# A vision tower with two experts per token: where the experts' rows are put in token order

## The reference, cut to what matters

```
x = _ln(mv + x, ln2_g, ln2_b)
logits = x @ gate_w + gate_b
topv, topi = jax.lax.top_k(logits, 2)
probs = jax.nn.softmax(topv, axis=-1)
w = jnp.sum(jax.nn.one_hot(topi, 8) * probs[..., None], axis=-2)
h = jax.nn.gelu(jnp.einsum('bsd,edf->ebsf', x, e_w1) + e_b1)
ye = jnp.einsum('ebsf,efd->ebsd', h, e_w2) + e_b2
moe = jnp.einsum('ebsd,bse->bsd', ye, w)
x = _ln(moe + x, ln3_g, ln3_b)
```

## Time and profile before

| | us |
|---|---|
| median of the runs (3329.47 to 3344.37) | 3334.4 |
| the profiled execution | 3318.28 |
| its span, first to last instruction | 3316.4 |
| TensorE busy (matmul) | 2775.0 |
| TensorE weight loads | 2181.5 |
| DVE busy | 1901.2 |
| ScalarE busy | 1843.2 |
| POOL busy | 1134.6 |

### The profile page before, as it was taken

How to read it: one execution, slowest core, us unless ns; L and a number is a source line. 1 busy time by engine, 2 the same in 40 slices (tenths; PEclk the granted TensorE clock), 3 DMA queues, 4 the chain that set the end, 5 groups by cost and what they waited for, 6 DMA issues and landing times.

```text
span 3316.4 us, 69976 instructions
## 1 busy us (share of the span) xinstructions
PE 2775.0 (84%) x25687; PEld 2181.5 (66%) x25687; DVE 1901.2 (57%) x4527; ACT 1843.2 (56%) x3725; POOL 1134.6 (34%) x964
## 2 busy tenths in 40 slices
PE   6999999999999859999996677877788777877787
PEld 4766666666666549999995456655566555655565
DVE  4878878878788742222221355655565555655566
ACT  4777777777777734444443345544454444544454
POOL 1454555655555530000002533333333333333310
PEclk9999999999999979999998688887888888878888
DMA  3222222222222137777774111111111111111110
GB/s 119 88 84 72 96 83 72 101 78 75 100 76 73 42 114 228 228 230 227 230 228 140 34 40 41 29 41 44 44 40 27 43 44 43 40 28 44 44 30 26
DMA packets 139758, 287.14 MB, mean 87 GB/s; under 512 B 25440, under 2 KB 82784, under 8 KB 135392
## 3 DMA queue, kind: packets, MB, share of 16 engines
q1 hardware_dynamic: 114912, 245.68, 22.9%
q0 software_dynamic: 24576, 37.80, 4.2%
...
## 4 chain that ended last, share of the span: by engine, by line
PE 47%; issue 7%; another core or an unknown queue 4%; DVE 3%; ACT 1%; POOL 1%; DMA 0%; SPq 0%; DVEq 0%; ACTq 0%; POOLq 0%
PE psum L1174 8%; PE psum L1165 8%; PE psum L1538 7%; PE psum L1498 5%; PE psum L1555 3%; PE psum L1568 3%; PE psum L1523 2%; PE psum L1503 2%; PE psum L1580 2%; DVE qdiag L1837 1%; PE psum L1598 1%; PE psum L1156 1%; PE psum L1546 1%; DVE inv L1852 1%
## 5 line engine op out<-in xcount | busy, mean ns | idle before, releaser
L1466 POOL DMA_INDIRECT ycho<-expert_out,place x384 | 367.5, 957 | 1417.4 <-DVE place L1829 1309.7
L1208 ACT ACTIVATE hid<-psum,w_blk 128x256 f32<-128x256 f32 x608 | 269.1, 474 | 326.2 <-PE psum L1165 326.2
L1039 POOL DMA_INDIRECT expert_in<-rows,slot_i x384 | 392.3, 1022 | 133.2 <-issue 111.6
L1852 DVE RECIPROCAL inv<-psum 128x64 f32<-128x64 f32 x288 | 159.5, 554 | 464.7 <-remote 385.9
L1538 PE MATMUL psum<-keys,qdiag 64*64 64x80 f32 x4608 | 281.4, 256 | 124.1 <-issue 123.7
L1752 ACT ACTIVATE ex<-psum,smin 128x80 f32<-128x80 f32 x1152 | 282.2, 332 | 142.9 <-DVE smin L1845 135.8
L1538 PEld LDWEIGHTS psum<-keys,qdiag 64*64 64x64 f32 x4608 | 214.8, 148 | 211.1 <-issue 195.7
L502 PE MATMUL psum<-xn,w_in 128*128 128x288 f32 x1024 | 311.1, 429 | 39.6 <-DVE xn L861 10.2
L1174 PE MATMUL psum<-w_blk,hid 128*128 128x128 f32 x2432 | 296.6, 275 | 0.0
L1568 PE MATMUL psum<-ex_t,pair_ones 128*32 128x64 f32 x4608 | 137.8, 244 | 189.6 <-DVE half L1853 124.0
L1165 PE MATMUL psum<-x_t,w_blk 128*128 128x256 f32 x1216 | 289.5, 381 | 2.4 <-DMA w_blk<-w_exp_in 2.4
...
## 6 DMA issues: line engine op xcount, KB each, us to landing
w_blk<-w_exp_in SPq DMA_DIRECT2D x152, 578.0 KB, 3.8
...
rows_in<-expert_in SPq DMA_DIRECT2D x152, 128.0 KB, 2.3
expert_out<-rows_out SPq DMA_DIRECT2D x152, 128.0 KB, 3.0
...
```

Of the source, the lines that this page charges most:

```text
L1039: pool.indirect_dma_start(out=expert_in[:, :], out_offset=bass.IndirectOffsetOnAxis(ap=slot_i[z.s][:, n:n + 1], axis=0), in_=rows[z.s][:, ...
L1208: nc.scalar.activation(hid[b.s][:, c, :], HB[b.s][c % HK], ACT.Gelu_apprx_tanh, bias=w_blk[b.q][:, FF + FC * D + c:FF + FC * D + c + 1]).t ...
L1466: pool.indirect_dma_start(out=ycho[x.s][:, k, :], out_offset=None, in_=expert_out[:, :], in_offset=bass.IndirectOffsetOnAxis(ap=place[x.s] ...
L1852: v.reciprocal(inv[:], sum_bank()).then_inc(head_step, 1)
```

## The change

1. A row in `expert_in` grows from 128 to 132 floats: the token's number, its first expert, and its two weights stand behind the data. POOL writes the token number (a small operation ahead of each item's scatters) and also waits for the weights.
2. The ranks come from three products: DVE forms a running sum over the six groups (a scan in place of the reduction), and one product with it replaces five.
3. The table load at L688 is made once, ahead of the steps.
4. In the expert stage DVE works out for each row of a block its weight (`share`) and its place by token (`dest`: first choices, then second choices, then a dump area for unused rows), adds the bias into `sums_y` and scales into `rows_out` (two operations). POOL stores each block by two indirect DMAs of 128 rows of 512 bytes; SP no longer stores. SP's load of a block's rows also waits for `dest`.
5. In the last stage the rows lie in token order: SP loads them with two plain DMAs for each item, ahead of its other work of the step; POOL's gather and multiplication, DVE's `place`, and the `out_rows` chain are gone. POOL only adds.

The diff, cut to its core:

```diff
-        expert_in = nc.dram_tensor("expert_in", (E * REGION + BLK, D), F32, kind="Internal").ap()
-        expert_out = nc.dram_tensor("expert_out", (NB * BLK, D), F32, kind="Internal").ap()
+        expert_in = nc.dram_tensor("expert_in", (E * REGION + BLK, RW), F32, kind="Internal").ap()
+        expert_out = nc.dram_tensor("expert_out", (3 * tokens + 2 * BLK, D), F32, kind="Internal").ap()
...
             def ranks(z, bank):
 
-                pe.wait_ge(route_step, z.upto(ROUTE, 13))
+                pe.wait_ge(route_step, z.upto(ROUTE, 15))
                 if z.old(1):
                     pe.wait_ge(chosen_new, z.upto(1, 0))
                 dst = rank_bank(bank)
-                nc.tensor.matmul(dst, C("before")[0:G, :], picks[z.s][:], start=True, stop=False)
-                for g in range(NG - 1):
-                    nc.tensor.matmul(dst[:, g + 1:NG, :], C("ones")[0:G, 0:G],
-                                     picks[z.s][:, g:g + 1, :].to_broadcast([G, NG - 1 - g, E]),
-                                     start=False, stop=False)
+                nc.tensor.matmul(dst, C("before")[0:G, :], by_group(picks[z.s][:]), start=True, stop=False)
+                nc.tensor.matmul(dst, C("ones")[0:G, 0:G], by_group(upto_g[z.s][:]), start=False, stop=False)
                 nc.tensor.matmul(dst, C("ones")[0:G, 0:G], chosen[:].unsqueeze(1).to_broadcast([G, NG, E]),
                                  start=False, stop=True).then_inc(rank_done, 1)
...
         def a_scalar(act):
             a_prep_scalar(act)
             act.wait_ge(consts_ready, 4)
+            act.preload_act_table_set("gelu_apprx_tanh_and_others")
...
             def step(x, y, z, w):
 
 
-                act.preload_act_table_set("gelu_apprx_tanh_and_others")
...
         def route_pairs(v, z):
             s = z.s
             route_after(v, z, 12)
-            v.tensor_tensor(picks[s][:], pick1[s][:], pick2[s][:], ALU.add).then_inc(route_step, 1)
+            v.tensor_tensor(by_group(picks[s][:]), pick1[s][:], pick2[s][:], ALU.add).then_inc(route_step, 1)
             v.tensor_tensor(wexp[s][:], top2[s][:], top1[s][:], ALU.subtract).then_inc(route_step, 1)
             route_after(v, z, 13)
-            v.tensor_reduce(newly[s][:], picks[s][:].rearrange("p g e -> p e g"), AX_X, ALU.add
-                            ).then_inc(route_step, 1)
+            v.tensor_tensor_scan(upto_g[s][:], within[:], picks[s][:], 0.0, ALU.mult, ALU.add).then_inc(route_step, 1)
...
                 if z:
+                    if z.old(2):
+                        pool.wait_ge(scattered[z.s], 16 * 2 * NG * z.n)
+                    pool.tensor_scalar(rows[z.s][:, :, TOKEN], C("token")[0:G, :], float((2 * z.n + z.s) * T), None,
+                                       ALU.add).then_inc(token_ready, 1)
+                    hold(pool, token_ready, z.upto(1, 1))
                     hold(pool, rows_ready, z.upto(2, 2))
                     hold(pool, slots_ready, z.upto(1, 1))
+                    hold(pool, route_step, z.upto(ROUTE, ROUTE))
                     for choice in range(2):
...
-            def store(b):
-                hold(sp, rows_out_ready[b.s], b.k + 1)
-                sp.dma_start(expert_out[bass.DynSlice(b.n * BLK, BLK), :].rearrange("(p c) d -> p (c d)", c=CB),
-                             rows_out[b.s][:].rearrange("p c d -> p (c d)")).then_inc(block_stored[b.s], 16)
-
             for q in range(BR):
                 load(Block(0, q))
             with sp.Fori(1, GROUPS) as i:
                 for q in range(BR):
-                    store(Block(i - 1, q))
                     load(Block(i, q))
-            for q in range(BR):
-                store(Block(GROUPS - 1, q))
-            for s in range(2):
-                sp.wait_ge(block_stored[s], 16 * (NB // 2))
+
+        def b_pool(pool):
+            def store(b):
+                hold(pool, dest_ready[b.s], b.k + 1)
+                hold(pool, rows_out_ready[b.s], b.k + 1)
+                for c in range(CB):
+                    pool.indirect_dma_start(
+                        out=expert_out[:, :], out_offset=bass.IndirectOffsetOnAxis(ap=dest[b.s][:, c:c + 1], axis=0),
+                        in_=rows_out[b.s][:, c, :], in_offset=None).then_inc(block_stored[b.s], 16)
+
+            with pool.Fori(0, GROUPS) as i:
+                for q in range(BR):
+                    store(Block(i, q))
 
...
             def turn_in(b):
                 pe.wait_ge(r_landed[b.q], 16 * b.i + 16)
                 if not b.first():
-                    pe.wait_ge(rows_out_ready[b.s], b.k)
+                    pe.wait_ge(sums_ready[b.s], b.k)
                 for c in range(CB):
-                    last = nc.tensor.transpose(TB[b.s][:, c * 128:(c + 1) * 128], rows_in[b.q][:, c, :], C("ident"))
+                    last = nc.tensor.transpose(TB[b.s][:, c * 128:(c + 1) * 128], rows_in[b.q][:, c, 0:D], C("ident"))
                 last.then_inc(in_turned[b.s], 1)
...
+            def shares(b):
+                expert = w_blk[b.q][:, WCOLS - 1:WCOLS]
+                first_pick = rows_in[b.q][:, :, FIRST]
+                v.wait_ge(r_landed[b.q], 16 * b.i + 16)
+                v.wait_ge(w_landed[b.q], 16 * b.i + 16)
+                v.tensor_scalar(second[b.s][:], first_pick, expert, float(tokens), ALU.not_equal, ALU.mult
+                                ).then_inc(share_step[b.s], 1)
+                v.scalar_tensor_tensor(out=share0[b.s][:], in0=first_pick, scalar=expert, in1=rows_in[b.q][:, :, W0],
+                                       op0=ALU.is_equal, op1=ALU.mult).then_inc(share_step[b.s], 1)
+                v.scalar_tensor_tensor(out=share1[b.s][:], in0=first_pick, scalar=expert, in1=rows_in[b.q][:, :, W1],
+                                       op0=ALU.not_equal, op1=ALU.mult).then_inc(share_step[b.s], 1)
+                if b.s:
+                    v.tensor_scalar(unused[:], first_pick, 0.0, float(BLK), ALU.is_equal, ALU.mult).then_inc(unused_step, 1)
+                    v.wait_ge(unused_step, 2 * b.k + 1)
+                    v.wait_ge(share_step[b.s], 4 * b.k + 1)
+                    v.tensor_tensor(second[b.s][:], second[b.s][:], unused[:], ALU.add).then_inc(unused_step, 1)
+                    v.wait_ge(unused_step, 2 * b.k + 2)
+                if not b.first():
+                    v.wait_ge(block_stored[b.s], 16 * CB * b.k)
+                v.wait_ge(share_step[b.s], 4 * b.k + 3)
+                v.tensor_tensor(share[b.s][:], share0[b.s][:], share1[b.s][:], ALU.add).then_inc(share_step[b.s], 1)
+                v.tensor_tensor(dest[b.s][:], rows_in[b.q][:, :, TOKEN], second[b.s][:], ALU.add
+                                ).then_inc(dest_ready[b.s], 1)
+
             def block(b, final=False):
                 if not final:
                     take_in(following(b))
+                shares(b)
                 v.wait_ge(y_done[b.s], b.k + 1)
-                if not b.first():
-                    v.wait_ge(block_stored[b.s], 16 * b.k)
-                v.tensor_tensor(rows_out[b.s][:], YB[b.s].rearrange("p (c d) -> p c d", c=CB),
-                                w_blk[b.q][:, WCOLS - D:WCOLS].unsqueeze(1).to_broadcast([128, CB, D]), ALU.add
-                                ).then_inc(rows_out_ready[b.s], 1)
+                v.tensor_tensor(sums_y[b.s][:], YB[b.s].rearrange("p (c d) -> p c d", c=CB),
+                                w_blk[b.q][:, WCOLS - 1 - D:WCOLS - 1].unsqueeze(1).to_broadcast([128, CB, D]), ALU.add
+                                ).then_inc(sums_ready[b.s], 1)
+                v.wait_ge(share_step[b.s], 4 * b.k + 4)
+                v.wait_ge(sums_ready[b.s], b.k + 1)
+                for c in range(CB):
+                    last = v.tensor_scalar(rows_out[b.s][:, c, :], sums_y[b.s][:, c, :], share[b.s][:, c:c + 1], None,
...
                 still(t)
 
         def c_sync(sp):
+            for s in range(2):
+                sp.wait_ge(block_stored[s], 16 * CB * (NB // 2))
+
             def load(x):
                 if x.old(2):
                     hold(sp, h2_ready, x.upto(1, -1))
                 sp.dma_start(h1c[x.s][:], h1_dram[:, a_range(x.n, x.s)]).then_inc(h_landed[x.s], 16)
                 sp.dma_start(x2c[x.s][:], x2_dram[:, a_range(x.n, x.s)]).then_inc(h_landed[x.s], 16)
+                if x.old(2):
+                    hold(sp, ysum_step, x.upto(1, -1))
+                for choice in range(2):
+                    sp.dma_start(ycho[x.s][:, choice, :, :].rearrange("p g d -> p (g d)"),
+                                 expert_out[choice * tokens + (2 * x.n + x.s) * T:choice * tokens + (2 * x.n + x.s + 1) * T,
+                                            :].rearrange("(p g) d -> p (g d)", g=NG)).then_inc(gathered[x.s], 16)
...
@@ -1454,36 +1495,16 @@
                 sp.wait_ge(out_stored[s], 16 * ITERS)
 
         def c_pool(pool):
-            for s in range(2):
-                pool.wait_ge(block_stored[s], 16 * (NB // 2))
```

(20 more changed lines are left out.)

112 lines of the change are left out of this document (54 added, 58 removed).

## The result

| | before | after |
|---|---|---|
| median of four runs, us | 3335.1 (3329.5 to 3344.4) | 2971.6 (2967.4 to 2977.2) |
| the profiled execution, us | 3318.3 | 2971.0 |

The ratio is 0.891, 95% interval 0.888 to 0.893: 11% faster. The forecast was 3010 us, with a range from 2865 to 3170. Against the profiled execution the sum had 2997 us, and that execution took 2971.

A forecast was written before the change was run, and what follows sets the result against it. TensorE was taken as the bound, busy throughout the expert stage and held back by POOL's strings of indirect DMAs elsewhere. 3318.3 - 418 - 17 + 0 + 114 = 2997, with 16 for the median 3013, given as 3010 us; range 2865 to 3170.

The forecast's parts named there:

- Last stage, steady steps: 29 steps of the last stage lose their gathers and fall from 46.34 to 31.9 us each: -418 us.
- The mechanism: A string of POOL's indirect DMAs lets about 45 TensorE matmuls through, then holds TensorE until the string has landed.
- Into the last stage: From the last expert block to the first transposes, 12.2 us in place of 29.2: -17 us.
- First stage: 31 steps, 0.4 us saved on ranks against 0.4 us of scatter delay: 0, with cases of +10 and -12 us.
- between 0.15 us and 0.6 us, I take 0.4: First stage: delay of POOL's scatters by the small token operation and a wait, counted in full each step.
- "-0.4" for the ranks: First stage: three products in place of seven save 0.7 us, less 0.3 us for the later scan.
- the table load: First stage: the 1.28 us load has ScalarE's wait behind it while TensorE embeds the next item: 0.
- Expert stage: Two scatters per block make TensorE wait 1.5 us for every two blocks: +114 us, from 0 to 245.
- "fits": Expert stage: DVE's added 1.9 us beside its 0.85 us fits within the 3.73 us of a block.
- Rival A: Expert stage: TensorE isn't held, 0 in place of +114, whole 2899 us; chance 0.30.
- Rival C: Expert stage: TensorE stands still during each scatter, 643 us in place of 114, whole 3542 us, beyond 6.6 us per block; chance 0.07.

The follow-up runs named there:

- plain_in_before: The kernel before with only the last stage's twelve gathers per item replaced by two plain loads issued by SP: 2909.8 us, one run.
- intervals: The kernel after with twelve extra gathers per last-stage step, the fillers between them varied: 33.0 us a step at 1.62 us between starts, 44.0 at 1.40.
- token_early: The kernel after with POOL's token operation moved to the start of its step: 2940.3 us, first stage 34.96 us a step.
- six_each: The kernel after, token operation early, first stage varied every six items: unchanged 34.89 us a step, seven rank products 34.89, table load back 34.82, scatter pauses 35.36 and 35.8.
- sp_stores: The kernel after with SP's contiguous store in place of POOL's two scatters per block, DVE's work kept: 2901.7 us, 3.73 us a block.
- no_shares: The kernel after with the scatters kept but DVE's shares and scalings removed, output rows unweighted: 2940.6 us, 4.02 us a block.

## Why the prediction was right, and where not

*Last stage, steady steps* (-418): -422 measured; 31.78 us against 31.9, full clock, nothing late but TensorE itself. The reading of the earlier trace rows was right in its place and size, and `plain_in_before` isolates it: 13.1 of 14.6 us a step were the gathers. The forecast gave all of it to them; the other 1.5 us came with the multiplication and the row numbers, which went at the same time.

*The mechanism* ("I take about 45 matmuls per string", and then a wait for its end) fits the gap-free strings of the earlier trace rows and is wrong as a rule. It is the distance of the starts, as `intervals` shows, not the matmuls let through: at 1.62 us twelve gathers let a step's 530 matmuls through for 1.2 us. The rows of before could not tell this, since all their strings run at 1.23 us but for their first three or four gaps.

*Into the last stage* (-17): -15.2. POOL's addition starts 9.0 us after the last scatter's start, where the sum had 8.2: the landing took 2.3 us until SP's first load and not 3.0, the loads 6.7 and not 5.2. The rest, 0.9 us, lies between the last block's sum and the first scatter (1.8 us, not 0.9). The stage's fill won another 12.7 us, which the sum had left out: the first items' gathers were in it too.

*First stage* (0, bounds -12 to +10): +34, outside its bounds. The step that failed is "between 0.15 us and 0.6 us, I take 0.4" for POOL's token operation with its waits: it delayed the first scatter by 1.7 us and the step by 1.1. I had priced an operation on 96 x 6 elements by DVE's rows, and the wait for its result by a pause that had no result to wait for. That the delay counts because the logits follow the last scatter by 3.0 us held, as `token_early` shows: without the 1.7 us in front of the string the step is 1.3 us shorter. "-0.4" for the ranks was 0 (`six_each`); the table load was 0 as said.

*Expert stage* (+114, from 0 to 245): +70. The place and the cause were right (`sp_stores`), the size was not. The forecast let 45 matmuls through and had TensorE wait for the landing of every second pair. In `no_shares`, where DVE has only two small operations more, nearly every block is longer by the same 0.28 us, and results are late within the 26 matmuls of each; one pair follows the other at 2.6 or 3.4 us in most blocks of the kernel after, with POOL idle in between. The view that DVE's chain "fits" was right only without late results; 28 of the 70 us come with it.

*Rival A* (no hold with such matmuls) falls by `sp_stores`: 3.73 without scatters, 4.02 with them. The Trainium skill, SBUF — State Buffer, section SBUF: two separate sides, which it was held against, has TensorE's and ScalarE's ports wait on no one. By that rule no wait for a port would make them late; in the traces results come late with POOL's closely spaced DMAs (ScalarE at 0.92 us in place of 0.63) and on time without, and whether a port has to do with it they don't show. *Rival C* falls too: 4.20 us a block is far from 6.6. The total came near the forecast partly by luck: the first stage's miss (+34) and the expert stage's (-44) nearly cancel.
